# Two attention layers and two routed feed-forwards on one core: the causal mask of the last two batches of layer A added by TensorE, and one residual add moved ahead of the row sums in layer B

## What is computed

```python
def attn_a(x, wq, bq, wk, bk, wv, bv, wo, bo):          # 16 heads of 8 channels, causal
    q, k, v = proj(x, wq, bq), proj(x, wk, bk), proj(x, wv, bv)
    scores = einsum('bhqd,bhkd->bhqk', q, k) / sqrt(8)
    mask = triu(full((t, t), NEG), k=1)
    return einsum('bhqk,bhkd->bhqd', softmax(scores + mask), v) -> (b, t, d) @ wo + bo
...
x = x + attn_a(layernorm(x))
x = x + ffn(layernorm(x))        # 8 experts, the best 2 of each token, hidden 512, silu gate
x = x + attn_b(layernorm(x))     # 16 heads, no mask; scores shifted and scaled by norms of q, k and x
x = x + ffn(layernorm(x))
```

## Time and profile before

| | |
|---|---|
| median of 3 runs | 1226.25 us (1221.29 to 1228.07) |
| profiled execution: its own time | 1225.01 us |
| profiled execution: span of the trace | 1222.7 us |
| TensorE clock granted, mean over the span | 0.888 of full speed |
| busy over the span: PE, DVE, ACT, POOL | 85%, 62%, 55%, 44% |

### The profile page before, as it was taken

The page is one execution under the profiler, slowest core; times in us unless marked ns, Lnnn a source line. Parts: engine busy times, 40 slices in busy tenths (PEclk is TensorE's granted clock), DMA queues, the critical chain, the costliest instruction groups (busy, mean ns, idle before and its releaser), DMA issues.

```text
span 1222.7 us, 28728 instructions
## 1 busy us (share of the span) xinstructions
PE 1037.5 (85%) x9198; PEld 725.6 (59%) x9198; DVE 762.5 (62%) x2336; ACT 674.0 (55%) x1399; POOL 539.0 (44%) x1010
## 2 busy tenths in 40 slices
PE   2999999887889989999688789997877899999930
PEld 1444555453359989999334344443533799999930
DVE  5687878868547323456768888889686553334522
ACT  2466777553435445556278678886746444555520
POOL 2243444323841610355688644563817145014345
PEclk9998999885759989999589899999957899999975
DMA  6464444642116977888443423333212387889832
GB/s 154 91 141 133 101 103 107 178 113 63 58 49 191 276 217 220 255 265 240 111 101 104 89 55 97 90 83 78 63 26 88 99 239 239 240 252 276 262 112 67
DMA packets 201722, 175.02 MB, mean 143 GB/s; under 512 B 19812, under 2 KB 160616, under 8 KB 201576
## 3 DMA queue, kind: packets, MB, share of 16 engines
q1 hardware_dynamic: 193384, 156.41, 46.7%
q0 software_dynamic: 8192, 16.79, 4.6%
HBM read 122.99 MB, written 50.14 MB: 142 GB/s over the span
## 4 chain that ended last, share of the span: by engine, by line
PE 58%; DVE 15%; POOL 9%; issue 6%; DMA 3%; ACT 1%; SPq 1%; POOLq 0%; DVEq 0%; ACTq 0%
PE psS L1332 10%; PE psT L1339 10%; PE psO L313 6%; PE psO L1355 5%; PE psS L347 5%; PE psN L1355 5%; POOL xn L1236 4%; DVE mx L659 4%; PE psS L374 2%; PE psT L355 2%; PE psN L320 2%; POOL prow L731 2%; PE psM L271 2%; PE psO L954 1%; PE psM L1320 1%
## 5 line engine op out<-in xcount | busy, mean ns | idle before, releaser
L659 DVE TENSOR_REDUCE mx<-psS 128x3 f32<-128x384 f32 (+1 forms) x512 | 311.8, 617 | 120.6 <-PE psS L374 65.6
L347 PE MATMUL psS<-kst,qst 48*128 48x256 bf16 (+1 forms) x1024 | 201.4, 287 | 57.3 <-DVE mx L659 42.8
L546 ACT ACTIVATE pT<-psT,scb 128x512 f32<-128x512 f32 x256 | 194.0, 778 | 55.5 <-PE psT L355 54.3
L1395 DVE TENSOR_TENSOR hT<-sg,psT 128x512 f32<-128x512 f32 x142 | 97.5, 686 | 171.6 <-PE psT L1339 145.0
L355 PE MATMUL psT<-qst,kst 50*128 50x256 bf16 (+1 forms) x1024 | 194.9, 282 | 5.0 <-DMA qst<-scr_m 2.2
L1223 POOL DMA_INDIRECT xg<-xn,slot x128 | 123.5, 965 | 146.5 <-DVE ysb L1390 82.3
L775 POOL TENSOR_SCALAR_AFFINE_SELECT pT<-pT 128x256 f32<-128x256 f32 x256 | 103.8, 412 | 137.3 <-ACT pT L541 135.4
L347 PEld LDWEIGHTS psS<-kst,qst 48*128 48x128 bf16 x1024 | 67.1, 97 | 155.5 <-DVE mx L659 77.6
L1332 PE MATMUL psS<-xTt,wgc 128*128 128x128 f32 x1136 | 154.5, 280 | 2.9 <-issue 2.9
L541 ACT ACTIVATE pT<-psT 128x384 f32<-128x384 f32 x256 | 122.3, 490 | 60.4 <-PE psT L355 58.4
L1339 PE MATMUL psT<-xTt,wuc 128*128 128x128 f32 x1136 | 153.0, 279 | 0.8 <-DMA wuc<-in_L_ffn_Wu 0.8
(11 more groups left out here) (216 smaller groups left out, 1620.3 us busy)
## 6 DMA issues: line engine op xcount, KB each, us to landing
wgc<-in_L_ffn_Wg SPq DMA_DIRECT2D x142, 256.0 KB
wuc<-in_L_ffn_Wu SPq DMA_DIRECT2D x142, 256.0 KB
scr_part<-part SPq DMA_DIRECT2D x128, 128.0 KB, 2.1
qst<-scr_part SPq DMA_DIRECT2D x64, 192.0 KB, 3.6
kst<-scr_part SPq DMA_DIRECT2D x64, 192.0 KB, 4.6
xin<-xg SPq DMA_DIRECT2D x142, 64.0 KB
eo<-ysb SPq DMA_DIRECT2D x142, 64.0 KB
scr_part<-part SPq DMA_DIRECT2D x32, 192.0 KB, 1.9
```

The source lines that it names most:

```text
L347: return nc.tensor.matmul(ps[:, c0:c0 + n], q_[r64, t, q0], k_[r64, t, 0:n], start=(half == 0), stop=True, skip_group_check=True)
L546: nc.scalar.activation(pT[:, g % 8, 0:cols], psT[g % 2][:, 0:cols], ACT.Exp, scale=scb[r][:, 0, i:i + 1], bias=scb[r][:, 1, i:i + 1]).then ...
L659: nc.vector.tensor_reduce(mx3[:, u, 0:n, pos:pos + 1].rearrange("p a b -> p (a b)"), psS[h % 2][:, 0:kcols(L)].rearrange("p (a k) -> p a k ...
```

## The change

In layer A the mask of batches 14 and 15 (`MASKED` is 14, so steps 17 and 18) no longer comes from POOL. A second mask `tritb`, the transpose of `trib`, is built at the start, and a matmul with `identb` adds it to the diagonal blocks of psT behind the transposed scores of each head. For that the second matmul of the transposed scores no longer starts a group of its own (`start=False`) in layer A. `pv_quad` of these two batches waits for the exponentials instead of for POOL. POOL's scatters stay behind the exponential of the same heads.

In layer B, `residual(1)` moves ahead of `dve_rows` at h = 15.

```diff
+MASKED = B - 2
...
             def pv_quad(b, r, q):
-                after(pe, s["pT"], 16 * b + 4 * q + 4)
+                after(pe, s["pT"], 16 * (min(b, MASKED - 1) if L.causal else b) + (4 * q + 4 if b < MASKED or not L.causal else H))
+                if L.causal and b >= MASKED:
+                    after(pe, s["exp"], 16 * b + 4 * q + 4)
...
                     return nc.tensor.matmul(ps[:, c0:c0 + T - q0], k_[m64, t, half * P:half * P + P], q_[m64, t, q0:T],
-                                            start=True, stop=True, skip_group_check=True)
+                                            start=(half == 0 or not L.causal), stop=True, skip_group_check=True)
...
                 if T_:
                     last_t = scores_t(1)
+                    if L.causal and bT >= MASKED:
+                        diag = psT[1 - par][:, 0:3 * P].rearrange("p (a k) -> p a k", a=3)[:, 0:3:2, :]
+                        last_t = nc.tensor.matmul(diag, identb[:], tritb[:].unsqueeze(1).to_broadcast([P, 2, P]),
+                                                  start=False, stop=True, skip_group_check=True)
                     last_t.then_inc(s["ST"], 1)
...
+                if h == 15 and O_ and not L.causal:
+                    residual(1)
                 if h == 15 and P_ and not L.causal:
                     dve_rows(dve, L, j)
...
-                if h == 15 and O_:
+                if h == 15 and O_ and L.causal:
                     residual(1)
...
                     after(pool, s["exp"], 16 * bT + h + 1)
-                    d = pT[:, (h ^ 1) % 8, 0:384].rearrange("p (a k) -> p a k", a=3)[:, 0:3:2, :]
-                    nc.gpsimd.affine_select(out=d, in_=d, compare_op=ALU.is_ge, fill=0.0, base=0,
-                                            pattern=[[0, 2], [1, P]], channel_multiplier=-1).then_inc(s["pT"], 1)
+                    if bT < MASKED:
+                        d = pT[:, (h ^ 1) % 8, 0:384].rearrange("p (a k) -> p a k", a=3)[:, 0:3:2, :]
+                        nc.gpsimd.affine_select(out=d, in_=d, compare_op=ALU.is_ge, fill=0.0, base=0,
+                                                pattern=[[0, 2], [1, P]], channel_multiplier=-1).then_inc(s["pT"], 1)
...
             nc.gpsimd.memset(trib[:], 0.0).then_inc(s_const, 1)
-            pool.wait_ge(s_const, 2)
+            nc.gpsimd.memset(tritb[:], 0.0).then_inc(s_const, 1)
+            pool.wait_ge(s_const, 3)
...
+            nc.gpsimd.affine_select(out=tritb[:], in_=tritb[:], compare_op=ALU.is_ge, fill=NEG, base=0,
+                                    pattern=[[1, P]], channel_multiplier=-1).then_inc(s_const, 1)
```

More of the change, by code:

```diff
@@ L97, in build @@
         trib = sb("trib", [P, P], BF16)
+        tritb = sb("tritb", [P, P], BF16)
         ones_row = sb("ones_row", [1, T])
@@ L1764, in _ @@
             dve.wait_ge(s_lnA, 1)
-            dve.wait_ge(s_const, 4)
+            dve.wait_ge(s_const, 6)
             nc.vector.tensor_copy(identb[:], ident[:]).then_inc(s_const_dve, 1)
@@ L1779, in _ @@
         def _(pe):
-            pe.wait_ge(s_const, 4)
+            pe.wait_ge(s_const, 6)
             pe_setup(pe, LA)
```

## The result

| | before | after |
|---|---|---|
| median | 1224.78 us (1221.29 to 1228.07, 4 runs) | 1210.88 us (1207.59 to 1215.22, 4 runs) |
| profiled execution, its span | 1225.01, 1222.7 us | 1212.88, 1211.1 us |
| TensorE clock granted | 0.888 | 0.900 |

The ratio is 0.9898, with a 95% interval from 0.9852 to 0.9943: 1.0% faster, 13.9 us by the medians. The forecast was 1221.5 us with a range down to 1214.5. It was wrong: the gain came out larger than forecast.

The account below looks back on a forecast made before the run. The prediction saw PE waiting for POOL's selects in layer A's steps 17 and 18 and for DVE at layer B's borders. Its terms, -2.1 + 0.2 - 2.9 = -4.8 us from 1226.25, gave 1221.5 us, range 1214.5 to 1228.5.

Parts of the forecast that it names:

- nothing changes between 331.48 and 343.10: Layer A, step 18: DVE's work from normalise to residual covers PE's stalls there, so no time changes.
- all that follows shifts as a whole: Step 19 and the feed-forward's first tiles hang on PE and DVE and only shift with step 18.
- Step 17: -2.1 forecast: Layer A: POOL's 1.05 us wait goes, 16 mask matmuls at 0.17 us come, clock stays up; 19.61 to 17.5 us.
- the ordinary step less its projection: Layer A, step 17 at full clock without mask matmuls: 15.87 us less a 1.07 us projection, 14.8 us.
- rival 2: Step 17: the clock falls anyway, +2.4 in place of -2.1; -0.3 us in all, 1226.0; chance 0.25.
- Rival 4: Steps 17 and 18: 23 mask matmuls at 0.33 us cost more than the waits; 1231.5 or 1228.6; chance 0.10.
- Step 18: +0.2 forecast: Layer A, step 18: mask matmuls add +0.5 and +1.0 us, the last 1.34 us stall goes.
- The +0.5 us for three masks ahead of the cover: Step 18 up to DVE's start at 331.48: three or so mask matmuls on PE and ACT's path, +0.5 us.
- +1.0 - 1.34: Step 18 from 343.10: four masks at half clock in heads 12 to 15, +1.0 us; last stall, 1.34 us, goes.
- POOL and the start, nothing: POOL loses 32 selects, its scatters still wait for exponentials; 0.5 us added at the start is hidden; no change.
- Layer B: -2.9 forecast: Borders of layer B's steps: DVE's gap before L676 closes, 0.36 us at each of 8 borders.
- Rival 3: Layer B gives PE's wait for the residual in full, up to 9.3 us; 1215; chance 0.18.

Follow-up runs that it names:

- no_mask_2: After without the mask matmuls on the transposed scores of batches 14 and 15, rerun on the first kind of chip: 0.9862 (0.9825 to 0.9899) of before.
- after_third: After itself, unchanged, run again on a chip where before takes 1225.6 us: 0.9865 (0.9822 to 0.9908) of before.
- both_2: After with GpSimd's selects and TensorE's waits for them as well as the mask matmuls, rerun on the first kind of chip: 0.9943 (0.9913 to 0.9972) of before.
- aside_2: After with GpSimd's 32 selects put back on a buffer nobody reads, rerun on the first kind of chip: 0.9904 (0.9869 to 0.9939) of before.
- b_only_2: Before with only layer B's residual moved, rerun on the first kind of chip: 0.9951 (0.9925 to 0.9976) of before.
- pe15_2: After, but GpSimd masks batch 14 and TensorE batch 15 alone, rerun on the first kind of chip: 0.9927 (0.9898 to 0.9956) of before.
- b_only: Before with only layer B's residual moved, on the other kind of chip: 0.9943 (0.9912 to 0.9975) of before.
- pe15: After, but GpSimd masks batch 14 and TensorE batch 15 alone, on the other kind of chip: 0.9975 (0.9948 to 1.0003) of before.
- both: After with GpSimd's selects and TensorE's waits for them as well as the mask matmuls, on the other kind of chip: 0.9963 (0.9936 to 0.9989) of before.
- a_only: After with layer B's residual left where it stood before, on the other kind of chip: 1.0018 (0.9986 to 1.0049) of before.
- no_mask: After without the mask matmuls on the transposed scores of batches 14 and 15, on the other kind of chip: 0.9971 (0.9947 to 0.9995) of before.
- pe14: After, but TensorE masks batch 14 alone and GpSimd batch 15 again, on the other kind of chip: 0.9989 (0.9969 to 1.0009) of before.
- aside: After with GpSimd's 32 selects put back on a buffer nobody reads, on the other kind of chip: 0.9928 (0.9900 to 0.9956) of before.
- spaced: After with memsets on a buffer nobody reads between GpSimd's scatters, on the first kind of chip: 0.9865 (0.9819 to 0.9912) of before.
- after_again: After itself, unchanged, run again on the other kind of chip: 0.9968 (0.9941 to 0.9994) of before.

## Why the prediction was wrong, point by point

Three steps failed: in step 18 that nothing changes between 331.48 and 343.10, behind it that all that follows shifts as a whole, and in step 17 the size of a mask matmul. The points take them in the order of the prediction.

- **Step 17: -2.1 forecast, -4.1 measured; the mechanism was the one named, its terms too dear.** The clock stayed up in all of after's three traces on this kind of chip. What I called the ordinary step less its projection, 14.8 us, is 14.4 (no_mask_2). Sixteen mask matmuls cost 15.5 - 14.4 = 1.1 us, 0.07 each, not 0.17: under the floor of 0.11 that I had set from a matmul of its size. In PE's timeline above, L378 starts 0.12 us ahead of its neighbour with the same weights, so 0.12 is what one takes in a row; that PE had this to spare in part of the heads would explain the 0.07, but no run shows it. At half clock it is (7.26 - 6.02) / 4 = 0.31, from DVE's residual to the last products in after_third and no_mask_2.
- **What the wait was worth.** Where I priced POOL in step 17 (rivals 2 and 4), it was at the 1.05 us that the trace showed; the -2.1 didn't use that price. both_2 has masks, waits and full clock, and takes 18.5 - 15.5 = 3.0 us longer than after; aside_2, with selects but no waits, takes 15.5, so the 3.0 are the waits'. The earlier trace rows had it: the chain goes along POOL from 307.62 to 318.25, select, scatter, select. POOL set the pace, and half clock merely hid PE's later waits for it: the second was 0.19 us in before, and 1.41 in both_2.
- **The clock.** That the stall brings it down is not borne out as I put it. Of the traces with the waits for POOL in step 17, it fell in before, b_only_2 and pe15_2, and on the other kind of chip in b_only and pe15, and not in both_2 nor in both. The columns of the masks aren't needed to keep it up either: no_mask_2 has none, and 1.00. On the first kind of chip it fell where there were waits and no masks, and stayed up where the waits went, where the masks came, and where both happened. On the other kind it fell also without any wait for POOL, in a_only behind 2.33 us of idling for DVE, masks and all (rival 2 came true there), and in no_mask behind 1.85. The length of one wait doesn't decide: it stayed up behind waits of 1.27 us in pe14 and of 1.41 in both_2. What does is open. What the clock is worth in step 17 isn't shown in full, since no run has waits, no masks and full clock throughout: layer A is the same code in before and b_only_2, and the fall that came later in b_only_2 (0.91 over the step in place of 0.74) goes with 0.7 us less; both_2 is 1.1 us shorter than before, with the masks in it. Of the Trainium skill's rule on long gaps (TensorE: Matmul & The Clock Gate, part 1, "HAM oscillation"), these traces show falls behind waits of 1.05 to 2.33 us, short ones by that page.
- **Step 18: +0.2 forecast, -5.0 measured; here the step failed that says that nothing changes between 331.48 and 343.10.** The cover got shorter itself, by 1.5 us: DVE's operations no longer took longer beside POOL's selects. aside_2 shows it without any wait of PE for them. The +0.5 us for three masks ahead of the cover wasn't there either: that part got 0.3 shorter (3.59 to 3.29 us, and 3.23 in no_mask_2). The Trainium skill (SBUF — State Buffer, "SBUF: two separate sides") has the rule: VectorE and GpSimd take a shared pair of ports for a whole instruction, and the other "fully blocks". That page speaks of VectorE's two-port modes and of operations with two inputs from SBUF; the trace agrees in that the normalisations and L876 grew, and the statistics (2.40 and 2.41 us) didn't. The prediction hadn't weighed it at all.
- **The last four heads and the stall of 1.34 us.** +1.0 - 1.34 was forecast, and -0.16 measured (7.42 to 7.26): masks 1.24 in place of 1.0. So the stall that went was worth 1.40 us (7.42 to 6.02, the latter without masks); this term stood within 0.2 us.
- **Behind the last products: 0 forecast, -3.1 measured.** I let all that follows shift as a whole. In the seven traces of the table without selects in step 18 the clock came back there and the part took 10.2 to 11.6 us; in the five with selects it stayed at half and took 13.95. aside_2 is among the five without PE waiting for POOL once, so it isn't the stall that decides. Nor is it the selects as such: on the other kind of chip aside has them and the clock came back, and three kernels without them stayed at half. What decides is open.
- **POOL and the start, nothing:** on this kind of chip, yes. On the other, "its scatters still wait for exponentials" missed that they come closer together, from 1.58 to 1.27 us, and layer A's part was worth nothing there. Useless selects between them brought 5.6 us back; that it is the spacing which does it is argued, since spaced never ran on that kind, and on the first kind the same 1.27 us did no harm.
- **Layer B: -2.9 forecast.** An ordinary border gave 0.6 us where I had 0.36 (0.61 by the step, 0.58 from maximum to maximum). The bound was DVE, as forecast, but I read the bracketed gap only: another behind L678 has no bracket, and with no gap left the operations overlap by some 0.07 us each time. Nine of the fifteen steps got shorter, by 0.6 us or more each and 6.0 us together; the other six together took 3.2 longer, most of it (2.5) in the step of the gathers. The layer's net in the trace is 2.8, by chance my number. By b_only_2 against before the part is worth 0.49% (0.24 to 0.75), 6.0 us, and 0.57% on the other kind. Rival 3, the full wait of 9.3 us, isn't it: the wait of 0.76 went, and the step gained 0.61.
- **Rival 4, slower by dear mask matmuls:** its price of 0.33 at half clock was right (0.31), but it needed half clock throughout.

So the sum came out at a third of the gain on chips of the first kind (0.9865 to 0.9898), and by the same numbers nearly right on the other (0.9968, where 4.8 us are 0.9961), though not for its reasons: there layer B's part gave 0.57%, about all of it, and in layer A late results ate the gain of steps 17 and 18.

## What to carry to other kernels

An idle time read from a trace prices a wait only if the engine waited for isn't setting the pace: follow the chain, and count what that engine would take for the whole stretch. Taking an instruction off an engine also frees what it shares with its neighbour and moves its other instructions closer together; the first gave 1.5 us here, and with the second the whole gain of layer A was missing on one kind of chip. A gain of 1% wants more than one chip and one pair of traces.

## What the runs showed of the hardware

- GpSimd's affine_select on a buffer of its own made VectorE's twelve 128x128 normalisations take 4.10 us in place of 3.16, and a memset there 3.43 to 3.53.
- A matmul of 256 columns with the same identity weights as the next one cost 0.07 us of the step at full clock (15.5 against 14.4 us for 16 of them), and 0.31 at half (7.26 against 6.02 us for four).
- On two of the chips, scatters 1.27 us apart went with results of TensorE reaching ScalarE and VectorE 0.8 to 0.9 us late, and steps of 19.0 to 22.1 us in place of 15.8; the traces don't show by what. Those chips' traces also hold waits that the profile puts down to "remote", mostly in the feed-forwards, which those of the other kind don't.
- Behind one point of step 18 the clock came back or not with whether GpSimd did selects there, in 12 of 12 traces on one kind of chip (10.2 to 11.6 us without selects, 13.95 with them). On the other kind aside had selects and took 11.4 us, and a_only, after_again and no_mask had none and took 13.95.
- The granted clock fell from full to half behind waits of TensorE of 1.05 us (before) to 2.33 us (a_only), and stayed at full behind 1.27 us (pe14) and 1.41 us (both_2).
